# The reciprocal roots of four groups, made on VectorE by Newton steps

## The reference, cut to what matters

```python
def _layernorm(x, axis=-1, eps=1e-05):
    m = jnp.mean(x, axis=axis, keepdims=True)
    v = jnp.var(x, axis=axis, keepdims=True)
    return (x - m) / jnp.sqrt(v + eps)
...
    # _L0_ffn_ref: 8 experts, each token goes to the one with the largest logit
    idx = jnp.argmax(logits, axis=-1)
    ...
    ys = jax.nn.silu(x_ @ w_gate_s.T) * (x_ @ w_up_s.T) @ w_down_s.T   # a shared expert
    return (y + ys).reshape(b, t, c)
...
    x = x + 0.5 * ffn(_layernorm(x))
    x = x + attn(_layernorm(x))
    x = x + 0.5 * ffn(_layernorm(x))
```

## Time and profile before

| what | value |
| --- | --- |
| median of three runs (lowest, highest) | 328.67 us (323.37, 329.1) |
| the profiled execution | 329.47 us |
| its span in the profile | 327.7 us |
| TensorE matmul busy | 262.4 us (80%) |
| VectorE busy | 185.5 us (57%) |
| GpSimd busy | 185.2 us (57%) |
| ScalarE busy | 160.3 us (49%) |

### The profile page before, as it was taken

The page is one execution under the profiler, slowest core; times in us unless marked ns, Lnnn a source line. Parts: engine busy times, 40 slices in busy tenths (PEclk is TensorE's granted clock), DMA queues, the critical chain, the costliest instruction groups (busy, mean ns, idle before and its releaser), DMA issues.

```text
span 327.7 us, 6436 instructions
## 1 busy us (share of the span) xinstructions
PE 262.4 (80%) x1788; PEld 213.1 (65%) x1788; DVE 185.5 (57%) x722; ACT 160.3 (49%) x374; POOL 185.2 (57%) x268
## 2 busy tenths in 40 slices
PE   0898996498988898896499889976898969989750
PEld 0566664267987798864386657753598969989430
DVE  3448551574453545538999898727644525544362
ACT  3545431035664666523699668510456545656200
POOL 4488787321656665662447888774125566576500
PEclk9999999599999999999859979995999997999996
DMA  7941111132333331119000111111323333211189
GB/s 190 370 180 43 41 50 53 34 99 61 90 91 96 97 82 34 49 41 254 5 1 25 40 37 35 34 58 57 86 67 95 87 93 91 67 41 43 40 234 279
DMA packets 34996, 28.42 MB, mean 87 GB/s; under 512 B 4784, under 2 KB 31792, under 8 KB 34704
## 3 DMA queue, kind: packets, MB, share of 16 engines
q1 hardware_dynamic: 25328, 16.06, 17.5%
q0 software_dynamic: 4544, 9.45, 8.6%
q10 hardware_dynamic: 5088, 2.50, 2.6%
HBM read 15.37 MB, written 12.62 MB: 85 GB/s over the span
## 4 chain that ended last, share of the span: by engine, by line
PE 42%; POOL 11%; DVE 10%; another core or an unknown queue 10%; issue 8%; ACT 6%; DMA 6%; SPq 3%; POOLq 1%; ACTq 1%; DVEq 0%
PE bank L893 21%; PE bank L901 7%; POOL dispatched L334 5%; PE bank L816 4%; DMA ey<-returned 3%; PE bank L882 2%; ACT wgu L463 2%; PE bank L841 2%; PE bank L824 2%; POOL scale_f L323 2%; DVE xres L548 2%; DVE st_f L532 2%; PE bank L802 2%; ACT xsT L479 2%
## 5 line engine op out<-in xcount | busy, mean ns | idle before, releaser
L363 POOL DMA_INDIRECT returned<-ey,token x78 | 77.5, 993 | 52.7 <-DVE ey L747 35.7
L893 PE MATMUL bank<-xsT,wgu 128*128 128x128 f32 x624 | 85.8, 281 | 14.9 <-ACT xsT L479 9.6
L893 PEld LDWEIGHTS bank<-xsT,wgu 128*128 128x128 f32 x624 | 76.7, 194 | 19.6 <-ACT xsT L479 11.7
L334 POOL DMA_INDIRECT dispatched<-xn,slot x64 | 64.2, 1003 | 26.2 <-issue 17.2
L816 PE MATMUL bank<-xnT,gu 128*128 128x512 f32 x128 | 68.1, 662 | 1.2 <-issue 0.4
L747 DVE COPY ey<-bank 128x128 f32<-128x128 f32 x78 | 22.6, 290 | 64.0 <-PE bank L901 52.3
L485 ACT ACTIVATE eg<-bank 128x256 f32<-128x256 f32 x78 | 29.9, 383 | 47.3 <-PE bank L893 42.0
L436 ACT ACTIVATE sg<-bank 128x512 f32<-128x512 f32 x32 | 19.0, 593 | 69.1 <-PE bank L816 30.0
L463 ACT ACTIVATE wgu<-gu 128x512 f32 x78 | 48.4, 625 | 3.5 <-issue 3.4
L901 PE MATMUL bank<-wdn,eh 128*128 128x128 f32 x312 | 48.2, 278 | 1.8 <-DVE eh L742 1.5
L901 PEld LDWEIGHTS bank<-wdn,eh 128*128 128x128 f32 x312 | 41.5, 194 | 2.4 <-DVE eh L742 1.9
(11 more groups left out here) (96 smaller groups left out, 290.2 us busy)
## 6 DMA issues: line engine op xcount, KB each, us to landing
xs<-dispatched SPq DMA_DIRECT2D x80, 66.0 KB, 1.9
ey<-returned SPq DMA_DIRECT2D x16, 256.0 KB, 5.1
gu<-in_gu SPq DMA_DIRECT2D x1, 2048.0 KB
out<-xres ACTq DMA_DIRECT2D x8, 256.0 KB, 5.0
returned<-ey,token POOLq DMA_INDIRECT x78
dn<-in_dn SPq DMA_DIRECT2D x1, 1024.0 KB
dispatched<-xn,slot POOLq DMA_INDIRECT x64
dispatched<-pads SPq DMA_DIRECT2D x10, 66.0 KB
```

The lines of the kernel that those rows point to most:

```text
L334: nc.gpsimd.indirect_dma_start(dispatched[:, :], bass.IndirectOffsetOnAxis(slot[:, i:i + 1], 0), xn[:, i, :], None, bounds_check=last_row) ...
L363: nc.gpsimd.indirect_dma_start(returned[:, :], bass.IndirectOffsetOnAxis(token[:, b:b + 1], 0), ey[:, b, :], None, bounds_check=last_back) ...
L893: last = nc.tensor.matmul(bank[4 + b % WR][:, i * P:(i + 1) * P], wgu[:, b % WR, i * P:(i + 1) * P], xsT[:, b // 2 % 2, b % 2, :], start=T ...
```

## The change

The reciprocal roots of groups 4 to 7 of the first normalisation are no longer made group by group on GpSimd. VectorE makes them all at once: a first guess from the bits of the variance, and three Newton steps, on a tile of 128 x 16. For that the statistics of groups 5, 6 and 7 are made earlier. The rest of the kernel is as before, but for counts that semaphores wait for.

```diff
--- before.py
+++ after.py
@@ -50,6 +50,9 @@
 
 ROUTE_STEPS = 7
 RSTD_STEPS = 2
+LATE_ROWS = 4
+SQRT_MAGIC = 0x5F3759DF
+NEWTON = 3
 N_CONST = 9
 N_TABLE_CONST = 5 + BU
 
@@ -105,6 +108,8 @@
         scale = {k: sb("scale_" + k, [P, NT]) for k in "fa"}
         shift = {k: sb("shift_" + k, [P, NT]) for k in "fa"}
         scale_more = sb("scale_more", [P, NT])
+        guess = sb("guess", [P, LATE_ROWS * TPG], I32)
+        step_y = sb("step_y", [P, LATE_ROWS * TPG])
 
 
         top = sb("top", [P, TPG])
@@ -169,6 +174,7 @@
         bn_done = {k: sem("bn_done_" + k) for k in "fa"}
         stats = {k: sem("stats_" + k) for k in "fa"}
         rstd_done = {k: sem("rstd_done_" + k) for k in "fa"}
+        newton, late_rstd = sem("newton"), sem("late_rstd")
         normed = {k: sem("normed_" + k) for k in "fa"}
         turned = {k: sem("turned_" + k) for k in "fa"}
         xnT_ready = sem("xnT_ready")
@@ -245,6 +251,14 @@
                 row = eng.value_load(pad_row[0:1, e:e + 1], min_val=0, max_val=E * CAP - P)
                 eng.dma_start(dispatched[bass.ds(row, P), :], pads[:, e, :]).then_inc(pad_sent, 16)
 
+        def by_newton(kind, n):
+
+            return kind == "f" and G - LATE_ROWS <= n < G
+
+        def rstd_count(kind, n):
+
+            return (n - LATE_ROWS if kind == "f" and n >= G else n) * RSTD_STEPS
+
         def wait_pos(eng, s, value):
 
             if value > 0:
@@ -321,7 +335,7 @@
                 pool.wait_ge(stats[kind], n + 1)
                 sc = cols(scale[kind], k)
                 nc.gpsimd.tensor_tensor(sc, cols(var[kind], k), minus_half[:], ALU.pow).then_inc(s, 1)
-                pool.wait_ge(s, n * RSTD_STEPS + 1)
+                pool.wait_ge(s, rstd_count(kind, n) + 1)
                 if kind == "a":
                     nc.gpsimd.tensor_tensor(cols(scale_more, k), sc, minus_one[:], ALU.subtract)
                 nc.gpsimd.tensor_tensor(cols(shift[kind], k), sc, cols(minus_mean[kind], k),
@@ -336,7 +350,7 @@
                         xn[:, i, :], None, bounds_check=last_row).then_inc(sent, 16)
 
             def first_ffn(k):
-                if valid(k + AHEAD):
+                if valid(k + AHEAD) and not by_newton("f", k + AHEAD):
                     rstd("f", k + AHEAD, k + AHEAD)
                 if valid(k):
                     scatter(0, k)
@@ -406,7 +420,10 @@
         def _(act):
             def norm(kind, n, k, dst, at):
 
-                act.wait_ge(rstd_done[kind], (n + 1) * RSTD_STEPS)
+                if by_newton(kind, n):
+                    act.wait_ge(late_rstd, 1)
+                else:
+                    act.wait_ge(rstd_done[kind], rstd_count(kind, n) + RSTD_STEPS)
                 for t in range(TPG):
                     i = k * TPG + t
                     nc.scalar.activation(dst[:, at * TPG + t, 0:C], xres[:, i, :], ACT.Identity,
@@ -543,6 +560,29 @@
                 nc.vector.tensor_scalar(cols(minus_mean[kind], k), m[:, :, 0], -1.0, None,
                                         ALU.mult).then_inc(stats[kind], 1)
 
+            def rstd_by_newton():
+
+                late = slice((G - LATE_ROWS) * TPG, NT)
+                v, y = var["f"][:, late], scale["f"][:, late]
+                steps_done = [0]
+
+                def link(ins):
+                    steps_done[0] += 1
+                    ins.then_inc(newton, 1)
+                    dve.wait_ge(newton, steps_done[0])
+
+                dve.wait_ge(stats["f"], G)
+                link(nc.vector.tensor_scalar(guess[:], v.bitcast(I32), 1, None, ALU.logical_shift_right))
+                link(nc.vector.tensor_scalar(y.bitcast(I32), guess[:], -1.0, float(SQRT_MAGIC), ALU.mult, ALU.add))
+                for i in range(NEWTON):
+                    link(nc.vector.tensor_tensor(step_y[:], y, y, ALU.mult))
+                    link(nc.vector.scalar_tensor_tensor(out=step_y[:], in0=step_y[:], scalar=-0.5, in1=v,
+                                                        op0=ALU.mult, op1=ALU.mult))
+                    link(nc.vector.scalar_tensor_tensor(out=y, in0=step_y[:], scalar=1.5, in1=y,
+                                                        op0=ALU.add, op1=ALU.mult))
+                nc.vector.tensor_tensor(shift["f"][:, late], y, minus_mean["f"][:, late],
+                                        ALU.mult).then_inc(late_rstd, 1)
+
             def add_half(k, what, done):
 
                 nc.vector.scalar_tensor_tensor(out=tiles(xres, k), in0=what, scalar=0.5, in1=tiles(xres, k),
@@ -625,6 +665,8 @@
                 n, q = f * G + k, k % 2
 
                 kind, later = ("f", k + AHEAD) if f == 0 else ("a", k + 4)
+                if f == 0 and k > G - LATE_ROWS - AHEAD:
+                    later = 2 * k + AHEAD - 1
                 if f == 0 and valid(later):
                     load = [i for i, (lo, hi) in enumerate(X_LOADS) if lo <= later < hi][0]
                     dve.wait_ge(x_in[load], 16)
@@ -639,6 +681,10 @@
                     stats_of("f", n + 2, k + 2)
                 if valid(k):
                     place_rows(n, k, q)
+                if f == 0 and k > 0 and k >= G - LATE_ROWS - AHEAD and valid(2 * k + AHEAD):
+                    stats_of("f", 2 * k + AHEAD, 2 * k + AHEAD)
+                    if 2 * k + AHEAD == G - 1:
+                        rstd_by_newton()
                 if k == G - 1:
                     pads_behind(f)
                 for g, part in parts_at(k, 1):
```

## The result

The changed kernel took 332.29 us (median of five runs, 330.72 to 333.3) beside 328.74 us for the kernel before in the same series: ratio 1.0176, 95% interval 1.01 to 1.0252. The ratios here leave out the slower runs of each kernel, while the medians are of all runs, so a ratio need not be the quotient of the medians. In a second series it was 1.0113 (1.0023 to 1.0203). Both intervals lie above 1: the change makes the kernel slower, by some one to two per cent. The time lies in the predicted range, but the forecast was a small gain, so the forecast was wrong; the rival that the insertion is not made good gave 332.0 us.

A forecast was written before the change was run, and what follows sets the result against it. VectorE's late last `choose` was taken to bound the first stage, with TensorE's signals held up behind GpSimd's scatters. Logits at 56.7 plus 2.6 gave 59.3 instead of 60.70, 1.4 us earlier: 327.3 us, range 322.0 to 332.5.

The forecast's parts named there:

- the rival that the insertion is not made good: Step 3 on VectorE: 3.3 us lost, signal at step 7 as late as before, 332.0 us; chance 0.27.
- What is added: On VectorE ahead of step 3: statistics 1.55 us and twelve Newton instructions 2.6 us, together 4.15 us, without slack.
- Two terms of the sum: At step 7: logits done at 56.7 us and reaching VectorE 2.6 us later, so last `choose` at 59.3.
- The disputed term: How late step 7's logits reach VectorE: 2.6 us instead of 7.27, half of four scatters' 5.1 us.
- TensorE's clock: Slower clock near step 3 or spared at the stage's end: counted at nothing, 1.7 us either way.
- The saving at the end: Shorter TensorE idleness at the stage's end could spare some of the 1.8 us lost to the lowered clock.
- Who waits: Around step 4: ScalarE's `norm` of group 4 adds nothing; TensorE's down matmuls start near 36.6 instead of 33.26 us.
- The rival that held: Step 3 on VectorE: 3.3 us not made good, step 7's signal as late as before, 332.0 us; chance 0.27.
- The rule on the shared port: VectorE instructions with two SBUF inputs block against GpSimd's SBUF reads, so Newton steps crawl beside scatters; the sum disregarded it.
- the rival that the prediction made of the rule: VectorE and GpSimd lock each other out in the Newton chain: 10.7 us more, 338 us; chance 0.03.

The follow-up runs named there:

- VectorE's part alone: Kernel before with the statistics moved and the Newton chain added on VectorE, writing to spare tiles, GpSimd keeping its powers: 332.25 against 329.36 us, 1.0097.

## Why the prediction was wrong, point by point

- **What is added** was right: 1.55 us of statistics (30.15 to 31.70 measured) and 2.4 us of Newton steps (31.73 to 34.13), 4.0 in all where 4.15 stood; the twelve are 0.21 us apart. VectorE has no slack there, as said.
- **Two terms of the sum failed.** The last `choose` was forecast at 59.3 and came at 66.13, 6.8 us later: the logits were done 4.0 us later than forecast (60.73 against 56.7), and their hold-up was 2.8 us longer (5.4 against 2.6).
- **The disputed term** was too small. The prediction put at most four scatters in front of the last logits. The longest row did shrink, from twelve to eight, and the hold-up with it, from 7.27 to 5.4 us; but it did not shrink to four, since the slots of groups 5 and 6 came 4.2 us apart and four scatters take 5.1. That does not come from the powers: VectorE's part alone has the same row with all of them kept. Where slots come in time, taking powers away even makes a new row (the wait of 5.83 us with the powers gone). The reading of the signals as held up behind scatters was right, and is now shown both ways: the waits at step 7 went when the scatters were moved, and when powers were put between them (0.995).
- **TensorE's clock** was counted at nothing, with 1.7 us either way. Behind the pause of 1.61 us and the slow transposes 10.2 us at half clock followed, which cost 3.6 us without scatters and 3.4 with. The prediction saw a pause of over 3 us (it came in three pieces, 1.61, 1.48 and 0.25), but took the clock's price from 7 us at 0.74; a stretch of 10.2 us at 0.50, full of matmuls, costs more. The saving at the end, which was to balance it, was small: the clock was 0.50 from 58.8 to 65.6 us with TensorE busy for 3.50 in the kernel before, and from 67.1 to 70.5 with 2.97 in the changed one.
- **Who waits.** `norm` of group 4 ended in time for the `mult` as forecast, but TensorE's transposes, which the prediction left out there, waited 1.61 us for it. With the 3.3 us of the insertion, 3.6 of the clock and 1.9 that lay ahead of step 2 in this execution, the last logits would come 8.8 us later; they came at 60.73, 7.3 later. The remaining 1.5 us weren't traced. The wait of 2.55 us ahead of step 5 has no counterpart now, and neither has the 0.99 us for which TensorE was idle ahead of these logits, just behind the late ranks of 52.06; together they are more than enough.
- **The rival that held** said that the hold-up at step 7 stays as long as it was, 332.0 us. Its number is right, in part by luck, and not for its reason alone: the hold-up fell by 1.9 us (7.27 to 5.4), and the half clock took more.
- **The rule on the shared port** would have had each Newton instruction wait for a scatter. They took 0.17 to 0.18 us beside the scatters of 31.78 to 35.31. The section that the prediction named, "SBUF — State Buffer" (Who interferes with whom) in the Trainium skill, also says that `tensor_tensor` did not stall DMA in its probe, and infers why. The rows agree with that (the scatters kept their 0.97 us too), and not with the rival that the prediction made of the rule.

## What to carry to other kernels

Before work is taken off an engine, ask what its instructions keep apart: here a power of 1 us between two groups of scatters was worth more than its time. Where a wait ends long after its signal was given, and 0.9 to 2.1 us after a row of scatters as here, suspect the row, and test it with a pause in it. An insertion on a path without slack costs its own time (3.9 us here), and once more what TensorE's clock does behind the pause that it makes (3.6 us). And before two profiles are compared, compare a point that lies ahead of the change.

## What was not expected

**When signals are held.** A row is here a run of scatters with pauses under 0.6 us:

| kernel | row of scatters (count) | TensorE done | after the row's start | used by VectorE | after the row's end |
| --- | --- | --- | --- | --- | --- |
| before, step 7 logits | 43.46 to 58.59 (12) | 53.43 | 10.0 | 60.70 | 2.1 |
| changed, step 6 ranks | 54.71 to 64.61 (8) | 58.06 | 3.4 | 58.25 | passed |
| changed, step 7 logits | the same | 60.73 | 6.0 | 66.13 | 1.5 |
| changed, step 5 ranks | 48.31 to 53.10 (4) | 52.65 | 4.3 | 54.02 | 0.9 |
| before, second pass | 211.59 to 221.58 (8) | 217.59 | 6.0 | 223.08 | 1.5 |
| before, step 6 ranks | 43.46 to 58.59 (12) | 49.53 | 6.1 | 52.06 | inside |
| powers gone, step 4 | 29.23 to 39.40 (8) | 36.90 | 7.7 | 40.75 | 1.35 |
| powers added, step 7 | 49.58 to 54.46 (4) | 51.27 | 1.7 | 51.30 | passed |
| changed, step 4 logits | 38.89 to 43.69 (4) | 43.65 | 4.8 | 43.68 | passed |
| before, second pass, step 2 ranks | 182.90 to 187.79 (4) | 185.67 | 2.8 | 188.78 | 1.0 |

In most of these lines a signal that TensorE gives in the first three to four microseconds of a row passes, and a later one is held until 0.9 to 2.1 us after the row's end. Three lines don't fit: the ranks of step 6 in the kernel before got through inside a row, the logits of step 4 in the changed kernel passed 4.8 us into one, and in the second pass ranks given 2.8 us into a row were held, though VectorE was busy for most of that time, until 187.81. So the time since the row's start does not decide alone. A row of four costs a signal up to 3.1 us in these lines, rows of eight and twelve up to 7.3. Why it is TensorE's signals, and what they queue behind (GpSimd's work on the scatters, or their transfers), no run here shows.

ScalarE's waits for TensorE end late in the same way. These are its first SiLUs after the row, in the kernel before and in the changed one; their matmuls were done at 55.25 and 62.54:

```profile
60.76 0.60 ACT L436 ACTIVATE sg<-bank 128x512 f32<-128x512 f32 x1 [10.68 <-remote]
```

```profile
66.19 0.60 ACT L453 ACTIVATE sg<-bank 128x512 f32<-128x512 f32 x1 [7.59 <-remote]
```

**A start of the full clock that varies.** The four matmuls at 18.72 took 3.76 us in the changed kernel's profile, and in that of before, 1.96:

```profile
18.29 1.96 PE L816 MATMUL bank<-xnT,gu 128*128 128x512 f32 x4
```

Step 2 then starts 1.9 us later (26.16 against 24.27). The granted clock reads 1.00 in both stretches, but in the changed kernel there is no reading behind that: the first record of the clock in the trace, at full clock, starts at 22.7 us there and at 17.8 in the kernel before. The late start is no part of the change. In all sixteen profiles the first record starts either at 16.3 to 17.8 us, and step 2 at 23.4 to 24.3, or at 22.0 to 23.0, and step 2 at 25.8 to 26.3. Both groups hold kernels with an untouched VectorE (the kernel before itself in the first, the kernel before with held scatters in the second) and kernels with the insertion (five and five). What decides it, and how much of the spread of the runs it makes, was not measured.
